# An attention and expert tower on one core: the order of work in its first stage (queries, keys and values)

## What is computed

```python
h = take(weight, ids)                      # rows of a table of 8000 x 256
x = (h - mean(h)) / sqrt(var(h) + 1e-5)    # layer norm of each row
ct_q, ct_kv = x @ Wd_q_w + Wd_q_b, x @ Wd_kv_w + Wd_kv_b       # latents, width 128
query = ct_q @ Wu_q_w + Wu_q_b + rope(ct_q @ Wq_r_w + Wq_r_b)  # "content" + "rotary"
key   = ct_kv @ Wu_k_w + Wu_k_b + rope(x @ Wk_r_w + Wk_r_b)
value = ct_kv @ Wu_v_w + Wu_v_b
# rope on pairs: out0 = x0*cos - x1*sin, out1 = x1*cos + x0*sin
```

## Time and profile before

| what | value |
|---|---|
| median of 3 runs | 3317.59 us (3316.93 to 3318.27) |
| the profiled execution's own time | 3315.87 us |
| span that its profile covers | 3314.0 us |
| busy in the span | TensorE 3202.7, VectorE 2908.6, ScalarE 2468.7, GpSimd 565.3 us |
| mean granted clock of TensorE | 0.986 of full |
| the first stage | from 0 to about 284 us, 16 chunks |

### The profile page before, as it was taken

How to read it: one execution, slowest core, us unless ns; L and a number is a source line. 1 busy time by engine, 2 the same in 40 slices (tenths; PEclk the granted TensorE clock), 3 DMA queues, 4 the chain that set the end, 5 groups by cost and what they waited for, 6 DMA issues and landing times.

```text
span 3314.0 us, 67613 instructions
## 1 busy us (share of the span) xinstructions
PE 3202.7 (97%) x27520; PEld 1369.7 (41%) x27520; DVE 2908.6 (88%) x3157; ACT 2468.7 (74%) x4578; POOL 565.3 (17%) x752
## 2 busy tenths in 40 slices
PE   7997999999999999999999999999999999986999
PEld 3443333333333333333333333333333333365666
DVE  6889999999999999999999999999999999567222
ACT  3331888888888888888888888888888888943221
POOL 7882000000000000000000000000000000046233
PEclk9997999999999999999999999999999999998999
DMA  6895213131313131313131313122222220168773
GB/s 201 256 299 159 54 49 72 37 72 37 72 38 72 38 74 38 72 40 72 37 72 39 83 34 79 39 70 44 65 45 58 45 83 21 37 204 305 231 238 101
DMA packets 269155, 305.40 MB, mean 92 GB/s; under 512 B 45270, under 2 KB 198399, under 8 KB 265517
## 3 DMA queue, kind: packets, MB, share of 16 engines
q1 hardware_dynamic: 256812, 271.63, 29.7%
q0 software_dynamic: 12032, 29.45, 2.7%
HBM read 165.81 MB, written 139.23 MB: 92 GB/s over the span
## 4 chain that ended last, share of the span: by engine, by line
PE 81%; ACT 4%; DVE 3%; issue 2%; POOL 1%; DMA 0%; another core or an unknown queue 0%; SPq 0%; POOLq 0%; DVEq 0%
PE ps_o L916 33%; PE ps_s L899 26%; PE ps_m L868 13%; ACT probs L1012 2%; PE ps_g L1592 2%; PE ps_y L1603 2%; PE ps_u L1592 2%; DVE max_parts L1027 2%; ACT weighted L992 1%; PE ps_td L1581 1%; ACT rows_c L1343 1%; POOL slot_rows L1257 0%; PE ps_s L883 0%; POOL shift_c L1234 0%; DVE stats_c L1377 0%
## 5 line engine op out<-in xcount | busy, mean ns | idle before, releaser
L1027 DVE TENSOR_REDUCE max_parts<-ps_m 128x2 f32<-128x1024 f32 x2048 | 2486.1, 1223 | 79.9 <-PE ps_m L868 71.5
L1012 ACT ACTIVATE probs<-ps_s 128x512 f32<-128x512 f32 x4096 | 2217.5, 597 | 312.3 <-PE ps_s L899 127.8
L868 PE MATMUL ps_m<-keys,queries 48*128 48x512 f32 x4096 | 1483.5, 453 | 17.1 <-DVE max_parts L1027 16.7
L899 PE MATMUL ps_s<-queries,keys 51*128 51x512 f32 x4096 | 1480.5, 447 | 9.5 <-ACT probs L1012 3.1
L916 PE MATMUL ps_o<-probs,vals 128*32 128x256 f32 x16384 | 1295.5, 391 | 0.0
L899 PEld LDWEIGHTS ps_s<-queries,keys 51*128 51x128 f32 x4096 | 610.5, 185 | 832.2 <-issue 785.2
L868 PEld LDWEIGHTS ps_m<-keys,queries 48*128 48x128 f32 x4096 | 595.4, 187 | 77.4 <-DVE max_parts L1027 50.2
L916 PEld LDWEIGHTS ps_o<-probs,vals 128*32 128x32 f32 x16384 | 329.4, 108 | 720.4 <-issue 699.0
L824 POOL TENSOR_TENSOR heads_out<-weighted,recip_rows 128x512 f32<-128x512 f32 x63 | 80.9, 1285 | 2147.4 <-DMA recip_rows<-recip_rows_dram 2147.4
L1663 DVE TENSOR_TENSOR hidden<-ps_u,silu 128x320 f32<-128x320 f32 x64 | 31.5, 492 | 127.4 <-PE ps_u L1592 101.6
L1639 ACT ACTIVATE silu<-ps_g 128x320 f32<-128x320 f32 x64 | 28.0, 438 | 134.1 <-PE ps_g L1592 82.8
(11 more groups left out here) (108 smaller groups left out, 1600.0 us busy)
## 6 DMA issues: line engine op xcount, KB each, us to landing
slot_rows<-empty SPq DMA_DIRECT2D x16, 1290.0 KB, 5.2
vext<-val SPq DMA_DIRECT2D x64, 256.0 KB
halves_q<-parts SPq DMA_DIRECT2D x64, 256.0 KB
halves_k<-parts SPq DMA_DIRECT2D x64, 256.0 KB
keys<-halves_k SPq DMA_DIRECT2D x32, 512.0 KB, 7.5
queries<-halves_q SPq DMA_DIRECT2D x128, 128.0 KB, 3.2
vals<-vext SPq DMA_DIRECT2D x32, 512.0 KB, 5.6
recip_rows<-recip_rows_dram SPq DMA_DIRECT2D x64, 256.0 KB
```

The lines of the kernel that those rows point to most:

```text
L868: mm = pe.matmul(ps_m[m % 2][:, h, :], queries_r[par][rows, qt, p, t * P:(t + 1) * P], keys_r[par][rows, p, c * 512:(c + 1) * 512], start= ...
L899: pe.matmul(ps_s[bank][:], keys_r[par][rows, p, k * P:(k + 1) * P], queries_r[par][rows, qt, p, :], start=True, stop=True).then_inc(scores ...
L1012: act.activation(probs[:, n % RING, :], ps_s[bank][:], ACT.Exp, scale=SCALE).then_inc(probs_ok[bank], 1)
L1027: dve.tensor_reduce(max_parts[:, lu % 2, :, p, t, c], ps_m[m % 2][:], AX.X, ALU.max).then_inc(maxima_ok[m % 2], 1)
```

## The change

All of it lies in `phase_a`, but for one count of a semaphore in the third stage.

- VectorE writes the keys' two sine terms into `ps_r` parts 0 and 1, in place of the rotary results that it read them from, and the cosine terms into a small buffer `terms_k` in SBUF. The keys' two sums then each read one input from SBUF and one from PSUM. TensorE's next rotary matmuls of the queries wait for these sums instead of the terms.
- VectorE now makes var + eps and minus mean itself, by two operations with one tensor input (`root_inputs`); GpSimd's `root` keeps the power and the product.
- VectorE's moments move to right behind the queries' terms; its statistics move from the chunk two ahead to the one three ahead, and stand in front of the keys' `full` instead of in front of their terms.
- GpSimd issues the gathers in front of the queries' sums; the rest of the keys moves behind the next chunk's `root`, and ScalarE's split of the keys behind the next chunk's first copy.
- TensorE transposes the next chunk in front of the queries' content (but in the first chunk).
- SyncE stores gathered rows, and loads the ids that follow, two chunks sooner.

```diff
--- before.py
+++ after.py
@@ -227,14 +227,13 @@
         rstd = sb("rstd", [P, 4, CT])
         neg_half = sb("neg_half", [P, CT])
-        eps_sb = sb("eps_sb", [P, CT])
-        no_mean = sb("no_mean", [P, CT])
         neg_mean = sb("neg_mean", [P, 4, CT])
         shift = sb("shift", [P, 4, CT])
...
         normed_t = sb("normed_t", [P, 2, KD, CH])
         lat = sb("lat", [P, 2, 2, CH])
-        terms = sb("terms", [P, 2, 4, CH])
+        terms = sb("terms", [P, 1, 4, CH])
+        terms_k = sb("terms_k", [P, 2, CH])
         sums = sb("sums", [P, 2, 2, CH])
         full = sb("full", [P, 2, 2, CH])
@@ -317,17 +315,22 @@
                     heads.load_ones(sp, heads.keys)
+            def keep_rows(b, k):
+
+                sp.wait_ge(rows_in[k], b * (16 * CT) + 16 * CT)
+                if b < BATCH - 1:
+                    nxt = dram["ids"][bass.ds(b * CPB + (k + 4), 1)].rearrange("a p t -> (a p) t")
+                    sp.dma_start(ids[:, k, :], nxt).then_inc(ids_in[k], 16)
+                row = b * SEQ + k * CH
+                sp.dma_start(dram["emb"][bass.ds(row, CH)].rearrange("(t p) n -> p t n", p=P), emb[:, k]).then_inc(emb_out[k], 16)
+
             def chunk(b, k, last):
                 par = k % 2
-                if not last:
-
-                    sp.wait_ge(rows_in[k], b * (16 * CT) + 16 * CT)
-                    nxt = dram["ids"][bass.ds(b * CPB + (k + 4), 1)].rearrange("a p t -> (a p) t")
-                    sp.dma_start(ids[:, k, :], nxt).then_inc(ids_in[k], 16)
-
-                row = b * SEQ + k * CH
-                sp.wait_ge(rows_in[k], b * (16 * CT) + 16 * CT)
-                sp.dma_start(dram["emb"][bass.ds(row, CH)].rearrange("(t p) n -> p t n", p=P), emb[:, k]).then_inc(emb_out[k], 16)
+                if (b, k) == (0, 0):
+                    keep_rows(0, 0)
+                    keep_rows(0, 1)
+                if not (last and k + 2 >= CPB):
+                    keep_rows(*((b, k + 2) if k + 2 < CPB else (b + 1, k + 2 - CPB)))
                 sp.wait_ge(val_ok, after(b, k, 2))
                 for t in range(CT):
@@ -360,19 +363,18 @@
             def root(b, k):
-                pool.wait_ge(stats_ok, after(b, k, CT))
-                pool.tensor_tensor(var_eps[:, k, :], mv[:, k, :, 1], eps_sb[:], ALU.add).then_inc(eps_ok, 1)
-                pool.tensor_tensor(neg_mean[:, k, :], no_mean[:], mv[:, k, :, 0], ALU.subtract).then_inc(neg_mean_ok, 1)
                 pool.wait_ge(eps_ok, after(b, k))
                 pool.tensor_tensor(rstd[:, k, :], var_eps[:, k, :], neg_half[:], ALU.pow).then_inc(rstd_ok, 1)
                 pool.wait_ge(rstd_ok, after(b, k))
-                pool.wait_ge(neg_mean_ok, after(b, k))
                 pool.tensor_tensor(shift[:, k, :], neg_mean[:, k, :], rstd[:, k, :], ALU.mult).then_inc(shift_ok, 1)
+            def rest(b, k, x):
+
+                pool.wait_ge(high_ok[x], after(b, k))
+                pool.tensor_tensor(parts[:, k % 2, x, 1].bitcast(F32R), full[:, x], parts[:, k % 2, x, 0], ALU.subtract).then_inc(low_ok[x], 1)
+
             pool.memset(neg_half[:], -0.5).then_inc(half_set, 1)
-            pool.memset(eps_sb[:], EPS).then_inc(half_set, 1)
-            pool.memset(no_mean[:], 0.0).then_inc(half_set, 1)
-            pool.wait_ge(half_set, 3)
+            pool.wait_ge(half_set, 1)
             for k in range(2):
                 pool.wait_ge(ids_in[k], 16)
@@ -389,25 +391,24 @@
                     pool.wait_ge(emb_out[ahead[1]], ahead[0] * 16)
                     pool.wait_ge(ids_in[ahead[1]], ahead[0] * 16 + 16)
+                    gather(*ahead)
                 pool.wait_ge(terms_ok[0], after(b, k, 4))
...
                 pool.tensor_tensor(sums[:, 0, 0, :], terms[:, 0, 0, :], terms[:, 0, 1, :], ALU.subtract).then_inc(sums_ok[0], 1)
                 pool.tensor_tensor(sums[:, 0, 1, :], terms[:, 0, 2, :], terms[:, 0, 3, :], ALU.add).then_inc(sums_ok[0], 1)
-                if ahead:
-                    gather(*ahead)
-                for x in range(2):
-                    if x == 1 and not (last and k + 2 >= CPB):
-                        root(*((b, k + 2) if k + 2 < CPB else (b + 1, k + 2 - CPB)))
-
-                    pool.wait_ge(high_ok[x], after(b, k))
-                    pool.tensor_tensor(parts[:, k % 2, x, 1].bitcast(F32R), full[:, x], parts[:, k % 2, x, 0], ALU.subtract).then_inc(low_ok[x], 1)
+                if not (last and k + 2 >= CPB):
+                    root(*((b, k + 2) if k + 2 < CPB else (b + 1, k + 2 - CPB)))
+                if (b, k) != (0, 0):
+                    rest(*((b, k - 1) if k else (b - 1, CPB - 1)), 1)
+                rest(b, k, 0)
             for b in range(BATCH - 1):
...
             for k in range(CPB):
                 chunk(BATCH - 1, k, True)
+            rest(BATCH - 1, CPB - 1, 1)
         @block.tensor
@@ -432,7 +433,7 @@
                 if x == 0:
-                    pe.wait_ge(terms_ok[1], b * (CPB * 4) + k * 4)
+                    pe.wait_ge(sums_ok[1], b * (CPB * 2) + k * 2)
                     pe.wait_ge(lat_ok, after(b, k, 2))
                 else:
@@ -470,9 +471,12 @@
                 nxt = (b, k + 1) if k + 1 < CPB else (b + 1, 0)
                 rotary(b, k, 0)
+                early = more and (b, k) != (0, 0)
+                if early:
+                    transpose(*nxt)
                 content(b, k, 0)
                 values(b, k)
-                if more:
+                if more and not early:
                     transpose(*nxt)
                 rotary(b, k, 1)
@@ -524,10 +528,11 @@
                 if more:
                     copy_nt(*nxt)
+                if (b, k) != (0, 0):
+                    split(*((b, k - 1) if k else (b - 1, CPB - 1)), 1)
                 split(b, k, 0)
                 if more:
                     copy_lat(*nxt)
-                split(b, k, 1)
                 if not (last and k + 2 >= CPB):
                     normalise(*((b, k + 2) if k + 2 < CPB else (b + 1, k + 2 - CPB)))
@@ -536,6 +541,7 @@
             for k in range(CPB):
                 chunk(BATCH - 1, k, True)
+            split(BATCH - 1, CPB - 1, 1)
         @block.vector
@@ -548,14 +554,30 @@
                     dve.bn_aggr(mv[:, k, t, :], stats[:, k, t, :]).then_inc(stats_ok, 1)
+            def root_inputs(b, k):
+                dve.wait_ge(stats_ok, after(b, k, CT))
+                dve.tensor_scalar(neg_mean[:, k, :], mv[:, k, :, 0], -1.0, None, ALU.mult)
+                dve.tensor_scalar(var_eps[:, k, :], mv[:, k, :, 1], EPS, None, ALU.add).then_inc(eps_ok, 1)
+
             def rope_terms(b, k, x):
                 pos = slice(k * CH, (k + 1) * CH)
...
                 if x == 0:
                     dve.wait_ge(sums_ok[0], b * (CPB * 2) + k * 2)
-                for n, (eo, tab) in enumerate(((0, cos_sb), (1, sin_sb), (1, cos_sb), (0, sin_sb))):
-                    dve.scalar_tensor_tensor(terms[:, x, n, :], ps_r[:, eo, :], b_cols[:, 2 + 4 * x + eo:3 + 4 * x + eo],
+                    dsts = [terms[:, 0, n, :] for n in range(4)]
+                else:
+                    dsts = [terms_k[:, 0, :], ps_r[:, 0, :], terms_k[:, 1, :], ps_r[:, 1, :]]
+                order = ((0, cos_sb), (1, sin_sb), (1, cos_sb), (0, sin_sb)) if x == 0 else \
+                        ((0, cos_sb), (0, sin_sb), (1, cos_sb), (1, sin_sb))
+                for dst, (eo, tab) in zip(dsts, order):
+                    dve.scalar_tensor_tensor(dst, ps_r[:, eo, :], b_cols[:, 2 + 4 * x + eo:3 + 4 * x + eo],
                                              tab[:, pos], ALU.add, ALU.mult).then_inc(terms_ok[x], 1)
+
+            def key_sums(b, k):
+
+                dve.wait_ge(terms_ok[1], after(b, k, 4))
+                dve.tensor_tensor(sums[:, 1, 0, :], terms_k[:, 0, :], ps_r[:, 1, :], ALU.subtract).then_inc(sums_ok[1], 1)
+                dve.tensor_tensor(sums[:, 1, 1, :], terms_k[:, 1, :], ps_r[:, 0, :], ALU.add).then_inc(sums_ok[1], 1)
             def add_content(b, k, x):
@@ -567,18 +589,24 @@
             dve.memset(val[:], 1.0).then_inc(ones_set, 1)
-            row_stats(0, 0)
-            dve.wait_ge(stats_raw, CT)
-            row_moments(0, 0)
-            row_stats(0, 1)
-            dve.wait_ge(stats_raw, 2 * CT)
-            row_moments(0, 1)
+            for k in range(2):
+                row_stats(0, k)
+                dve.wait_ge(stats_raw, (k + 1) * CT)
+                row_moments(0, k)
+                root_inputs(0, k)
             dve.wait_ge(const_in, 16 * NCONST)
             dve.wait_ge(tables_in, 32)
...
             def chunk(b, k, last):
                 rope_terms(b, k, 0)
+                ahead = None if last and k + 2 >= CPB else (b, k + 2) if k + 2 < CPB else (b + 1, k + 2 - CPB)
+                if (b, k) == (0, 0):
+                    row_stats(*ahead)
+                if ahead:
+                    dve.wait_ge(stats_raw, after(*ahead, CT))
+                    row_moments(*ahead)
+                    root_inputs(*ahead)
```

(28 more changed lines are left out.)

## The result

| what | before | after |
|---|---|---|
| median of the runs | 3318.27 us (3316.39 to 3322.39, 11 runs) | 3297.35 us (3295.82 to 3315.72, 11 runs) |
| the profiled execution's own time | 3315.87 us | 3296.17 us |
| span that its profile covers | 3314.0 us | 3294.4 us |
| busy: TensorE, VectorE, ScalarE, GpSimd | 3202.7, 2908.6, 2468.7, 565.3 us | 3198.9, 2903.6, 2465.9, 546.4 us |
| mean granted clock of TensorE | 0.986 | 0.986 |

The ratio of times, after to before, is 0.9945, 95% interval 0.9935 to 0.9954: 15.3 to 21.6 us saved. The medians lie 20.9 apart, more than the ratio's 18.3, since three of the eleven executions after took 4 to 18 us more than the median, at a lower mean clock (3301.71 at 0.984, 3305.63 at 0.983, 3315.72 at 0.979). The forecast was 3298.

A forecast was written before the change was run, and what follows sets the result against it. A closed circle of GpSimd and VectorE was taken to hold chunks at 16.00 us against TensorE's 14.67. Savings 20.8 + 0.9 less 2.3 (key loads 2.0, gaps 0.3) gave 19.4: 3296.5 profiled, 3298 median, range 3294 to 3306.

The forecast's parts named there:

- The circle: First stage: GpSimd's round and VectorE's held first keys' sum wait on each other, making chunks 16.00 us instead of 14.67.
- The pace after: First-stage chunks come down to TensorE's limit of 14.67 us; 13 chunks save 20.8 us.
- The PSUM writes: VectorE's keys' terms written to PSUM take 0.70 to 0.75 us each; upper end 2.12, as the held sum.
- The two small operations: Var + eps and minus mean on VectorE take 0.16 us each, hidden under the values.
- the rule set against the change: VectorE's single-input fp32 SBUF operations take both read ports, so they and GpSimd's operations lock each other out.
- VectorE takes over: Rival, 0.15: both GpSimd sums hold the new small operations, values begin at 7.5, chunks take 14.95 us; 3302 us.
- The last chunk: First stage's last chunk: the keys' `full` ends at 14.4 us instead of 15.27, saving 0.9.
- The start of the stage: Earlier gathers delay the first sums some 1.4 us, hidden because the first keys' terms wait for statistics; cost 0.
- The key loads: First stage: key loads choke the queues 14 us, delaying late halves' stores and a gather; 2.0 us charged, between 0 and 4.4.
- DMA sets the pace: Rival, 0.05: the 16.0 us chunks are the DMA engines' pace, so nothing happens; about 3317 us.
- The share of 0.39: DMA engines' load falls to 0.39 within a chunk; used against rivals where DMA sets the pace or stores land late.
- A circle through the late stores: Rival, 0.06: late stores of the keys' halves hold ScalarE's split two chunks on; 16.85 us a chunk, 3324 us.

The follow-up runs named there:

- experiment 1: The kernel after, with the keys' terms back in SBUF, so both sums read two SBUF inputs: 3301.57 us, ratio 0.9945.
- experiment 2: The kernel before, with only the keys' terms put in PSUM and TensorE waiting for the sums: 3303.16 us, ratio 0.9953.
- control: The kernel after itself, unchanged, run again on another chip: 3296.52 us, ratio 0.9923 to the kernel before.
- experiment 9: The kernel after, with var + eps and minus mean on GpSimd and its constant fills behind the first chunk's rest: 3296.56 us, ratio 0.9925.
- experiment 7: The kernel after, with var + eps and minus mean back on GpSimd: 3296.07 us, ratio 0.9947.
- experiment 8: The kernel after, with GpSimd's five fills of constants moved behind the first chunk's rest: 3294.89 us, ratio 0.9949.
- experiment 10: The kernel after, with each chunk's gathered rows stored a second time, 0.52 MB more per chunk: 3302.86 us, ratio 0.9951.
- experiment 5: The kernel after, with rows stored and ids loaded in their own chunk as before: 3362.32 us, ratio 1.0152.
- experiment 3: The kernel after, with the keys' split and rest back in their own chunk: 3366.28 us, ratio 1.0138.
- experiment 11: The kernel with both small edits (fills later, small operations on GpSimd), plus unused TensorE matmuls early in the second stage: 3309.33 us, ratio 0.997.

## Why the prediction was right, point by point

- **What bound the kernel.** Right. The circle went through the held sum: put back, it costs 0.28 us a chunk even in the new order (experiment 1); taken out alone, it brings 14.7 of the 21 us (experiment 2).
- **The pace after.** 14.67 foreseen, 14.62 measured, with no member of VectorE's or GpSimd's schedule off by more than 0.3 us but for the small operation below and the start of the values behind it (t = 6.0, foreseen 5.55).
- **The PSUM writes.** 0.70 to 0.75 taken, 0.75 measured; the upper end, 2.12, never came near.
- **The two small operations.** This step of the sum failed: 0.16 each was taken from the earlier trace rows, and L559 took 1.05 (mean 0.89 over the stage). It ends with GpSimd's sum (107.43 and 107.40), and with only a gather of GpSimd's beside it (32.58 to 33.53), in the first chunk at 33.41, it takes 0.17. So the rule set against the change is borne out: "VectorE: DVE Perf Modes" of the Trainium skill (the perf-mode tier table, with Mode 2x_2P) and its "SBUF - State Buffer" (two separate sides) say that such an operation and GpSimd shut each other out. It cost no time, because the values behind it had slack. "VectorE takes over" was thus right in its mechanism; its price was lower, since as a rule only the first sum holds L559: the values then begin at t = 6.0 and not 7.5. At 7.5 the sum would have been 3302.
- **The last chunk.** `full` ends at t = 14.4, as foreseen; 0.9 gained.
- **The start of the stage.** Foreseen at 0, measured 1.21 us of TensorE's wait: the first chunk took 16.07 us, where before it took 42.69 - 28.00 = 14.69. That the second chunk starts only 0.1 later is luck: the first latents in front took 5.42 us in this execution and 6.47 before, and they took 5.1 to 6.5 in the executions profiled, whatever the kernel. The first chunk's keys' terms do not wait for statistics any more, but the first sums come only at 34.80, behind fills and two rounds of gathers, and VectorE's `full` of the queries waits for them. I had excused that delay with a wait that the change itself removes.
- **The key loads.** 2.0 charged, nothing paid in this execution. The late stores did delay ScalarE's split of the queries, the one that I named: it began at 170.32 - 159.89 = 10.4 us of its chunk instead of 8.8. That is 1.7 late, GpSimd's rest behind it lost 0.39, and GpSimd's idle 1.26 us took that up. In the next four chunks it began at t = 10.6, 10.0, 10.6 and 9.4, and TensorE never saw it. Other executions did pay a little: the same chunk took 14.93 us in the control, 15.09 in experiment 9's other kernel and 15.24 in experiments 7 and 8, so 0.3 to 0.6. With the 0.3 for gaps this charge is why the first stage gave 22.1 instead of 19.4.
- **The total.** 3296.5 was forecast for the profiled execution and 3296.17 came. Two errors hide in that: 2.7 us more gained in the first stage, and 2.3 lost in the second, where nothing was changed. The control's profiled execution, on another chip, has nearly the same two marks (first reduction at 261.90, last `ps_o` at 2893), so it is no chance of one execution; what it is stays open. That the forecast was met to 0.3 us is in part luck.
- **The rivals that did not come.** *DMA sets the pace* fell by experiment 10, and yet my reason against it was bad. The share of 0.39 is a valley of 4 us; over whole chunks of before it is 0.82 to 0.94 away from the key loads (0.82 for 90.64 to 106.64), and now 0.92. There was room for the 0.5 MB more that experiment 10 moved beside 4.2 (290 GB/s for 14.62 us), but not for the 60% that I argued from. *A circle through the late stores* did not close here, though its wait is there in five chunks; with 0.52 MB more it did (experiment 10). What makes a slower kernel out of these parts is another circle: the rows' store (experiment 5) or the keys' rest (experiment 3) in front of the gathers.

**What each part is worth**, measured by its absence: keys' terms in PSUM about 4 us where the rest is new (13 chunks of 0.28) and 14.7 alone; the transposes' place about 2 (0.17 in 13 chunks, an estimate); the two small operations nothing that can be told; gathers in front, keys' rest a chunk later and rows stored early stand or fall together: any of the three undone costs 24 to 70 us, more than the whole change brings.

**Left open.** When the clock comes back in the second stage: about 51 us after its fall in most profiled executions, about 65 in experiment 7's, though that kernel does there just what the kernel after does. What decides it was not found. Nor was it found why the second stage ran 2.3 us longer.

## What to carry to other kernels

Where a closed circle of several engines sets the pace, look for the member that takes longer than the same instruction elsewhere in the trace (2.12 against 0.70 us here), and free that one first: one such edit brought most of this change. When work is moved ahead on one engine, list what has to arrive sooner for it (rows, stores, a half of the round before), since each of those, left where it was, cost more than the move gained. And take the load of the DMA engines over whole periods of the loop, never from a gap inside one.

## What the runs showed of the hardware that was not expected

- A VectorE operation on 4 elements a partition with one fp32 input was held as long as a large one: 1.05 us as a rule, 2.12 and 2.51 in the first two chunks of experiment 8, 2.43 once in the control, 0.17 beside a mere gather. Whether one or both of two back-to-back GpSimd sums hold it varied.
- The hold has a mirror: GpSimd's four-element operations went from about 0.65 to 0.20 us when VectorE's sum beside them had an input in PSUM (experiment 2).
- The DMA engines' share reached 1.02 at 323 GB/s for 45 us without delaying TensorE until a burst (the key loads) came on top (experiment 10).
- The first latents take 5.1 to 6.5 us instead of 3.6, different in each execution, while the granted clock reads 1.00 there. Why is not shown.
- A granted clock of 0.50 outlasted 65 us (265 to 330) in which TensorE was shown busy without a gap (experiment 11).
